# New orders of steps for four of the five blocks of a fused scan, attention and expert kernel

## The reference

```python
x = x + L0_conv(_gn(x))                 # group norm, in_proj, 3x3 depthwise conv, silu, selective scan in 4 directions
t = tokens(x)
t = t + L1_attn(_ln(t))                 # causal attention, 12 heads of 16
t = t + L1_ffn(_ln(t))                  # a second norm, full attention, MLP 192-768-192, then a mixture of 4 experts, top 2
# inside the scan, for each of 4 directions, 96 channels, 16 states, 256 steps:
h = h * exp(d_t * A) + (d_t * u_t) * B_t
y = sum_n(h * C_t)
```

## Time and profile before

| | us |
|---|---|
| median of 3 runs (lowest, highest) | 740.43 (737.93, 743.23) |
| the profiled execution | 742.85 |
| its span in the trace | 741.1 |
| TensorE busy in the span | 608.1 (82%) |
| VectorE busy | 516.4 (70%) |
| ScalarE busy | 321.5 (43%) |
| GpSimd busy | 201.3 (27%) |

### The profile page before, as it was taken

How to read it: one execution, slowest core, us unless ns; L and a number is a source line. 1 busy time by engine, 2 the same in 40 slices (tenths; PEclk the granted TensorE clock), 3 DMA queues, 4 the chain that set the end, 5 groups by cost and what they waited for, 6 DMA issues and landing times. The chain is left out here.

```text
span 741.1 us, 9169 instructions
## 1 busy us (share of the span) xinstructions
PE 608.1 (82%) x3378; PEld 392.0 (53%) x3378; DVE 516.4 (70%) x986; ACT 321.5 (43%) x588; POOL 201.3 (27%) x158
## 2 busy tenths in 40 slices
PE   3899947898737689958898789867996989898897
PEld 2232225455212576645455576645465767676696
DVE  3869746868998578789997478799995465542311
ACT  2334202236353053784572345583761324672241
POOL 4449710005474201053442010153441001000000
PEclk9999968689768799878999789889999999999999
DMA  6375940348772002386750004575620000000000
GB/s 130 40 178 145 278 141 0 44 99 206 185 188 60 11 0 38 80 200 155 178 134 0 22 0 57 144 187 147 181 63 11 0 2 1 0 1 11 1 1 11
DMA packets 26642, 61.70 MB, mean 83 GB/s; under 512 B 4928, under 2 KB 12752, under 8 KB 26608
## 3 DMA queue, kind: packets, MB, share of 16 engines
q1 hardware_dynamic: 26608, 61.26, 34.8%
HBM read 53.52 MB, written 3.54 MB: 77 GB/s over the span
## 5 line engine op out<-in xcount | busy, mean ns | idle before, releaser
L1106 PE MATMUL pd<-w_dn,act 128*128 128x192 f32 x480 | 87.2, 336 | 5.5 <-ACT act L1872 3.7
L1992 POOL TENSOR_TENSOR state<-state,C_rows 128x1024 f32<-128x1024 f32 x24 | 69.8, 2909 | 62.5 <-DVE state L1491 40.6
L1106 PEld LDWEIGHTS pd<-w_dn,act 128*128 128x128 f32 x480 | 80.2, 195 | 11.7 <-issue 6.3
L1090 PE MATMUL pu<-fT,w_up 128*128 128x256 f32 x180 | 61.8, 427 | 7.6 <-ACT act L1872 7.6
L1967 POOL TENSOR_TENSOR norm_rstd<-norm_var,half 128x2 f32<-128x2 f32 x20 | 14.0, 698 | 197.5 <-DVE norm_var L1304 197.5
L1872 ACT ACTIVATE act<-pu,b_up 128x256 f32<-128x256 f32 x90 | 37.7, 470 | 67.4 <-PE pu L1094 67.2
L942 PE MATMUL py<-identb 128*32 128x512 bf16 x224 | 59.1, 412 | 0.0
L1842 ACT ACTIVATE decay<-d_rows,a_neg 128x255 f32<-128x255 f32 x96 | 40.5, 498 | 11.2 <-DVE state L1491 10.3
L1092 PE MATMUL pu<-fT_high,w_up_stack 128*128 128x256 f32 x90 | 45.2, 503 | 0.0
L1032 PE MATMUL py<-state,sel 128*32 128x512 f32 x96 | 43.8, 665 | 1.6 <-POOL state L1992 1.6
L822 PE MATMUL ps<-hT,w_qkv 96*96 96x256 f32 x128 | 35.9, 444 | 9.5 <-ACT hT L1902 8.6
(11 more groups left out here) (310 smaller groups left out, 1384.6 us busy)
## 6 DMA issues: line engine op xcount, KB each, us to landing
dx_rows<-delta_x_dram SPq DMA_DIRECT2D x41, 512.0 KB, 5.2
d_rows<-delta_dram SPq DMA_DIRECT2D x36, 512.0 KB, 6.3
d_rows<-delta_x_dram SPq DMA_DIRECT2D x6, 512.0 KB, 4.8
w_dn<-exp_w_dram SPq DMA_DIRECT2D x1, 2304.0 KB
B_rows<-xdbl SPq DMA_DIRECT2D x4, 512.0 KB, 6.9
C_rows<-xdbl SPq DMA_DIRECT2D x4, 512.0 KB, 10.5
delta_x_dram<-delta_x SPq DMA_DIRECT2D x4, 384.0 KB, 3.4
w_up<-exp_w_dram SPq DMA_DIRECT2D x1, 1536.0 KB
```

Of the source, the lines that this page charges most:

```text
L1090: nc.tensor.matmul(out, w_up[:, e, hidden], fT[:, :], start=True, stop=False)
L1106: mm = nc.tensor.matmul(pd[:, WIDTH * tl:WIDTH * (tl + 1)], act[e % 2][:, m, 128 * tl:128 * (tl + 1)], w_dn[:, e, m, :], start=(m == 0), s ...
L1992: nc.gpsimd.tensor_tensor(now, now, C_rows[:, :], ALU.mult).then_inc(sc_done, 1)
```

## The change

The lists of OPENING, FIRST, STEADY and LAST are written anew; CLOSING stays. No operation is changed. On VectorE, ScalarE and GpSimd the opening keeps its sequence, though the slots are named otherwise, and so does GpSimd in STEADY and LAST. The number of fillers goes from 23 to 28 in the opening, 121 to 76 in FIRST, 29 to 44 in STEADY and 17 to 13 in LAST. The core of the diff:

```diff
@@ -55,90 +55,94 @@
 OPENING = {
     "PE": {
...
-        (0, 1): [("keep_busy", 7)],
-        (0, 3): [("x_dbl", 0), ("x_dbl", 1), ("dt", 0), ("dt", 1), ("keep_beside", 9), ("spread_delta", 0)],
-        (0, 4): [("keep_beside", 1), ("spread_delta_x",), ("spread_delta", 1)],
...
-        (1, 10): [("y_sum", 10), ("keep_beside", 4)],
...
-        (1, "context"): [("keep_beside", 2), ("y_norm",)],
...
+        (0, 1): [("group_sums",), ("in_proj",), ("keep_busy", 7), ("x_dbl", 0), ("x_dbl", 1),
+            ("keep_beside", 1), ("dt", 0)],
+        (0, 2): [("dt", 1), ("keep_beside", 10)],
+        (0, 3): [("spread_delta", 0), ("spread_delta_x",), ("spread_delta", 1)],
...
+        (1, 5): [("spread_delta", 11), ("y_sum", 8), ("y_sum", 9), ("keep_beside", 8)],
...
+        (1, 10): [("keep_beside", 2)],
...
 FIRST = {
     "PE": {
-        (0, "turned"): [("keep_busy", 5), ("x_turn",), ("keep_busy", 6), ("group_sums",)],
-        (0, "projected"): [("in_proj",)],
+        (0, "turned"): [("keep_busy", 6), ("x_turn",), ("keep_busy", 7), ("group_sums",)],
+        (0, 0): [("in_proj",)],
...
-        (0, 9): [("dt", 1)],
-        (0, 11): [("keep_busy", 5)],
-        (0, "spread"): [("keep_busy", 19)],
-        (0, "output"): [("keep_busy", 30)],
-        (1, "projected"): [("keep_busy", 12), ("y_sum", 0), ("keep_busy", 15)],
...
-        (1, 2): [("y_sum", 3), ("y_sum", 4), ("keep_busy", 13)],
-        (1, 3): [("keep_busy", 5)],
...
+        (0, 10): [("dt", 1)],
+        (0, "context"): [("keep_busy", 6)],
+        (0, "output"): [("keep_busy", 27)],
+        (1, 0): [("y_sum", 0)],
+        (1, 1): [("keep_busy", 13), ("y_sum", 1)],
+        (1, 2): [("y_sum", 2), ("keep_busy", 12)],
+        (1, 3): [("y_sum", 3), ("y_sum", 4)],
...
-        (1, 7): [("y_sum", 7), ("y_sum", 8), ("y_sum", 9)],
...
+        (1, 7): [("keep_busy", 5), ("y_sum", 8), ("y_sum", 9)],
...
-        (1, 10): [("keep_busy", 1), ("y_sum", 11), ("keep_busy", 10)],
+        (1, 10): [("y_sum", 11)],
...
     "ACT": {
...
-        (0, 9): [("softplus", 0)],
-        (0, 11): [("softplus", 1)],
-        (0, "context"): [("softplus_log",)],
-        (0, "spread"): [("split_up", 0)],
+        (0, 1): [("in_proj",), ("split_up", 0)],
...
+        (0, 5): [("x_dbl", 1), ("split_up", 1)],
+        (0, 8): [("split_up", 2)],
+        (0, 9): [("softplus", 0), ("softplus", 1)],
+        (0, "output"): [("softplus_log",)],
...
-        (1, "projected"): [("decays", 1), ("split_up", 1), ("decays", 2)],
...
-        (1, 1): [("decays", 5), ("decays", 6), ("split_up", 2), ("decays", 7)],
-        (1, 4): [("split_up", 3), ("decays", 8)],
-        (1, 5): [("split_up", 4)],
-        (1, 6): [("split_up", 5), ("decays", 9), ("decays", 10)],
...
+        (1, 4): [("split_up", 3), ("decays", 7), ("decays", 8), ("decays", 9)],
+        (1, 6): [("split_up", 4), ("split_up", 5), ("decays", 10)],
...
     "POOL": {
...
-        (0, "output"): [("split_up", 0), ("times_C", 0)],
...
-        (1, 2): [("times_C", 3), ("split_up", 1), ("times_C", 4)],
...
+        (1, 2): [("split_up", 0), ("times_C", 2)],
+        (1, 3): [("times_C", 3), ("split_up", 1)],
         (1, 4): [("split_up", 2)],
...
-        (1, 10): [("split_up", 3), ("times_C", 7)],
...
-        (1, "context"): [("y_norm",), ("split_up", 4)],
-        (1, "output"): [("y_out",), ("split_up", 5)],
...
+        (1, 6): [("split_up", 3), ("times_C", 5), ("times_C", 6)],
...
+        (1, 8): [("split_up", 4), ("split_up", 5)],
...
 STEADY = {
     "PE": {
-        (0, "turned"): [("ffn_turn", 0), ("keep_busy", 2), ("x_turn",)],
-        (0, "projected"): [("group_sums",)],
-        (0, 0): [("ffn_up", 0, 0)],
-        (0, 1): [("in_proj",), ("ffn_up", 0, 1)],
-        (0, 2): [("ffn_up", 0, 2), ("ffn_down", 0, 0), ("ffn_down", 0, 1)],
-        (0, 4): [("x_dbl", 0)],
-        (0, 5): [("x_dbl", 1), ("keep_busy", 5), ("ffn_turn", 1), ("dt", 0)],
-        (0, 6): [("ffn_up", 1, 0), ("ffn_logits",)],
-        (0, 7): [("ffn_up", 1, 1)],
-        (0, 8): [("ffn_turn_gates",), ("dt", 1)],
-        (0, "context"): [("ffn_bias",), ("keep_busy", 5)],
-        (0, "spread"): [("ffn_up", 1, 2)],
+        (0, "turned"): [("ffn_turn", 0), ("x_turn",)],
+        (0, "projected"): [("keep_busy", 3)],
+        (0, 0): [("group_sums",)],
+        (0, 1): [("ffn_up", 0, 0), ("in_proj",), ("ffn_up", 0, 1), ("ffn_up", 0, 2)],
+        (0, 2): [("ffn_down", 0, 0)],
+        (0, 3): [("ffn_down", 0, 1)],
+        (0, 4): [("x_dbl", 0), ("keep_busy", 5)],
+        (0, 6): [("x_dbl", 1)],
+        (0, 7): [("dt", 0), ("ffn_turn", 1)],
+        (0, 8): [("ffn_up", 1, 0), ("dt", 1), ("ffn_logits",)],
+        (0, 10): [("ffn_up", 1, 1)],
+        (0, "spread"): [("ffn_turn_gates",), ("keep_busy", 15), ("ffn_bias",), ("ffn_up", 1, 2)],
         (0, "output"): [("ffn_down", 1, 0), ("ffn_up", 2, 0), ("ffn_up", 2, 1)],
         (1, "turned"): [("ffn_up", 2, 2)],
-        (1, "projected"): [("y_sum", 0), ("y_sum", 1), ("ffn_up", 3, 0)],
+        (1, "projected"): [("ffn_up", 3, 0), ("y_sum", 0), ("y_sum", 1)],
         (1, 0): [("ffn_down", 1, 1)],
-        (1, 1): [("y_sum", 2), ("ffn_down", 2, 0)],
-        (1, 3): [("y_sum", 3)],
-        (1, 4): [("ffn_down", 2, 1), ("y_sum", 4), ("ffn_up", 3, 1), ("y_sum", 5)],
-        (1, 6): [("keep_busy", 6), ("ffn_up", 3, 2), ("y_sum", 6), ("y_sum", 7)],
-        (1, 7): [("y_sum", 8), ("ffn_down", 3, 0), ("ffn_down", 3, 1), ("ffn_up", 4, 0)],
-        (1, 8): [("keep_busy", 11), ("ffn_up", 4, 1), ("y_sum", 9), ("ffn_up", 4, 2)],
-        (1, 10): [("y_sum", 10), ("y_sum", 11), ("y_norm",)],
-        (1, 11): [("ffn_down", 4, 0)],
-        (1, "context"): [("y_turn",)],
-        (1, "spread"): [("y_out",), ("ffn_down", 4, 1)],
+        (1, 2): [("y_sum", 2), ("y_sum", 3), ("ffn_down", 2, 0), ("ffn_down", 2, 1)],
+        (1, 3): [("ffn_up", 3, 1), ("keep_busy", 10), ("y_sum", 4), ("y_sum", 5), ("ffn_up", 3, 2)],
+        (1, 4): [("y_sum", 6), ("y_sum", 7)],
+        (1, 5): [("ffn_down", 3, 0), ("keep_busy", 5), ("y_sum", 8), ("keep_busy", 6), ("ffn_down", 3, 1)],
+        (1, 6): [("ffn_up", 4, 0), ("y_sum", 9)],
+        (1, 7): [("ffn_up", 4, 1)],
+        (1, 8): [("ffn_up", 4, 2)],
+        (1, 10): [("y_sum", 10), ("y_sum", 11)],
+        (1, 11): [("y_norm",), ("ffn_down", 4, 0), ("ffn_down", 4, 1), ("y_turn",)],
+        (1, "context"): [("y_out",)],
     },
...
     "DVE": {
...
-        (0, 3): [("silu",), ("ffn_norm", 0)],
-        (0, 4): [("x_dbl", 0), ("ffn_norm", 1)],
...
-        (0, 7): [("ffn_logits",)],
-        (0, 11): [("dt", 1), ("ffn_turn_gates",), ("softplus", 0), ("softplus", 1)],
-        (0, "context"): [("softplus_log",)],
...
+        (0, 4): [("ffn_norm", 0), ("x_dbl", 0)],
+        (0, 6): [("ffn_norm", 1)],
...
+        (0, 9): [("dt", 1), ("softplus", 0)],
+        (0, 10): [("ffn_logits",)],
+        (0, 11): [("softplus", 1)],
+        (0, "context"): [("ffn_turn_gates",), ("softplus_log",)],
...
-        (1, 1): [("ffn_add", 1), ("scan", 5)],
-        (1, 3): [("scan", 6)],
...
-        (1, 5): [("scan", 8), ("ffn_add", 2)],
-        (1, 7): [("scan", 9), ("scan", 10), ("scan", 11)],
-        (1, 9): [("ffn_add", 3), ("y_copy",)],
-        (1, 11): [("y_norm",)],
...
-        (1, "spread"): [("y_out",), ("ffn_add", 4)],
...
+        (1, 2): [("ffn_add", 1)],
+        (1, 3): [("scan", 6), ("scan", 7), ("scan", 8), ("ffn_add", 2)],
+        (1, 4): [("scan", 9)],
+        (1, 5): [("scan", 10)],
+        (1, 7): [("ffn_add", 3), ("scan", 11)],
+        (1, 10): [("y_copy",)],
+        (1, 11): [("y_norm",), ("ffn_add", 4), ("y_turn",)],
...
     "ACT": {
...
-        (0, 8): [("ffn_logits",), ("ffn_up", 1, 1), ("softplus", 0)],
-        (0, "context"): [("softplus", 1), ("softplus_log",), ("ffn_up", 1, 2)],
-        (0, "spread"): [("ffn_up", 2, 0), ("decays", 0)],
-        (0, "output"): [("ffn_up", 2, 1), ("decays", 1), ("ffn_up", 2, 2)],
-        (1, "turned"): [("decays", 2), ("decays", 3)],
...
+        (0, 7): [("softplus", 0)],
...
+        (0, 9): [("softplus", 1), ("ffn_logits",)],
+        (0, 11): [("softplus_log",), ("ffn_up", 1, 1), ("ffn_up", 1, 2), ("ffn_up", 2, 0)],
+        (0, "context"): [("decays", 0), ("ffn_up", 2, 1), ("decays", 1)],
+        (0, "output"): [("decays", 2)],
+        (1, "turned"): [("ffn_up", 2, 2), ("decays", 3)],
         (1, "projected"): [("decays", 4)],
-        (1, 0): [("decays", 5), ("decays", 6)],
-        (1, 4): [("ffn_up", 3, 0), ("decays", 7), ("decays", 8)],
...
-        (1, 6): [("decays", 9), ("ffn_up", 3, 2)],
-        (1, 7): [("decays", 10), ("decays", 11), ("ffn_up", 4, 0)],
+        (1, 1): [("decays", 5), ("ffn_up", 3, 0), ("decays", 6), ("decays", 7)],
+        (1, 3): [("decays", 8), ("ffn_up", 3, 1), ("ffn_up", 3, 2), ("decays", 9)],
+        (1, 5): [("decays", 10), ("ffn_up", 4, 0), ("decays", 11)],
...
 LAST = {
     "PE": {
```

(32 more changed lines are left out.)

233 lines of the change are left out of this document (116 added, 117 removed).

## The result

The changed kernel takes 745.50 us (median of 7 executions, 742.64 to 746.83), the kernel before 741.89 in the same session. The ratio is 1.0051, 95% interval 1.0027 to 1.0074: slower by half a per cent, where 734 us and a gain of 6.8 were predicted. The profiled execution has a span of 743.7 us after 741.1 (745.43 us in all after 742.85).

A forecast was written before the change was run, and what follows sets the result against it. VectorE, taking turns with GpSimd in the scans, was taken as the bound over most of the span. Opening +0.3, first attention block -2.5, middle -3.6, last -1.0 sum to -6.8 us: 734 from 740.43, range 729 to 739.

The forecast's parts named there:

- First attention block, first half: First attention block up to its scan half: in_proj behind row_max 0 gives -1.3 us, moved fillers and earlier softplus 1 -1.0.
- Opening: Opening: fillers moved on TensorE around dt, the spreads and y_sum 10 cost +0.3 us, bounds -0.5 and +2.7.
- First block's scan half: First attention block's scans: more VectorE and GpSimd meetings, and possible waits for row maxima, cost +1.3 us.
- norm_shift: First attention block's end: with split_up moved away, two small operations run freed, norm_shift from 0.93 to 0.16 us; -1.5 us.
- Middle block, first half: Middle block ahead of its scan half: waits for logits and second transpose go, fillers nearly pay for themselves; -1.2 us per pass.
- Scan half 0: Middle block's scans: VectorE keeps its work and its cycle with GpSimd, decays 11 just fit; 0 us per pass.
- Tail: Middle block's end: output leaves before the layer norm, hiding its transfer, and the second ffn_down 4 costs 1.5; -0.6 us per pass.
- Middle block -3.6: Middle block as a whole: -1.8 us per pass, -3.6 for its two passes.
- A: Fifteen fillers ahead of the middle block's output projection run at 1.2 GHz; +3 us per pass, 740 us; chance 0.20.
- B: TensorE bounds the middle block's scan half, at shifted 1, making a late decay delay scan 11; 748 us, mildly 742; chance 0.14.
- C: Fewer meetings of VectorE and GpSimd in the first attention and middle blocks; -8 us, 726 us; chance 0.16.
- D: Whole kernel: a gain in one half is waited away at the next projection; 740 us; chance 0.08.

The follow-up runs named there:

- e4: Changed kernel with TensorE's order of the first attention block's first half as before, other engines' orders staying changed; 742.27 us, 0.9977 of the kernel before.
- e7: Changed kernel with eight more TensorE fillers in the first attention block's first half; 744.18 us, 1.0019 of the kernel before.
- e3: Changed kernel with only in_proj of the first attention block moved back ahead of the scores; 742.44 us, 1.0008 of the kernel before.
- e13: The kernel of e3 again, unedited, for a second profile; 746.13 us.
- e2: Kernel before with only the middle block of the changed kernel; 754.95 us, 1.0147 of the kernel before.
- e12: The kernel of e2 again, unedited, profiled in a later session on another chip; 745.91 us.
- e1: Changed kernel with the whole first attention block of the kernel before; 745.61 us, 1.0042 of the kernel before.
- e5: Changed kernel again, nothing edited, for a second profile; 747.27 us.
- e15: The kernel of e4 with, in the middle block, ffn_up 3,0 behind row_max 0 and in_proj ahead of ffn_up 0,0; 1.0091 of the kernel before.
- e16: The kernel of e7 with ffn_up 3,0 moved behind row_max 0 in the middle block; 739.69 us, 0.9968 of the kernel before.
- e18: The kernel of e16 again, unedited, for a tighter interval; 744.61 us, 1.0026 of the kernel before.
- e17: The kernel of e4 with ffn_up 3,0 behind row_max 0 in the middle block and the eight fillers of e7; 742.57 us, 1.0021 of the kernel before.

## Why the prediction was wrong

*The step that failed* is "First attention block, first half": -1.3 for in_proj, -1.0 for the rest, +5.0 measured. The two edges that it named did what it said. The third stack's copy starts at 120.76 where it was 120.72, although the block had begun 0.76 us and its x_turn another 0.6 later: the 1.3 us of in_proj are there. The wait of 2.35 us went. What failed is the silent assumption behind these sums, that TensorE's clock would be up where it was up before. in_proj, put behind row_max 0, ran at 1.2 GHz (1.91 + 1.86 us), z came 2.0 us later, and from there every step of the half but its end ran at the lower level. e4 and e7, in which the clock came back by 34 us of the block, show the half at 53.4 and 53.5 us. Why the clock misses its rise under the changed order in six of seven profiles stays open: in_proj put back alone (e3, e13) didn't bring it up. The clock appears in that paragraph once, as a bound of 2.1 us on the projection (0.5 measured), not on the 41 us ahead of it. The Trainium skill, page TensorE: Matmul & The Clock Gate, section "What's actually happening", says that the throttled state is the default, and that the monitor runs free of the kernel, so that the ramp varies from run to run. This case's profiles agree that one program varies (e2 against e12: 59.5 and 52.6 us for the half), and the prediction had used only the first of these two statements.

*The other terms.* Opening +0.3: +0.76 measured. First block's scan half +1.3: +1.08 measured, and the multiplies took 0.8 us more than in the earlier trace rows:

```profile
L1499 DVE TENSOR_TENSOR dx_rows<-dx_rows,B_rows 128x1024 f32<-128x1024 f32 x12 | 22.4, 1864 | 1.1 <-DMA dx_rows<-delta_x_dram 1.1
```

norm_shift -1.5: from y_copy to the end of the block 14.5 us for 16.0, so the gain came; but y_copy starts 6.1 us behind the last scan where it started 4.5 behind, with the wait of 1.45 us for row maxima in between that the sum had not counted, and the tail took +0.15. Middle block, first half, -1.2 a pass: +1.71 and -0.90. "0" for in_proj behind ffn_up 0,0 was mis-sized: VectorE waits 2.93 and 2.60 us for z where it waited 1.2 and 1.3. From z to the residual the passes gain 0.5 and 0.7 only: the 0.89 is gone, but 0.25 of the 0.45 stays, and in the first pass 0.62 us stand ahead of the last transpose, which waited for nothing, and 0.55 ahead of the multiply behind it. Scan half 0: -0.42 and -0.46 in this profile, about +2.5 a pass in half of the 26. Tail -0.6: -1.6 in both passes; hiding the transfer was worth 1.9 us of the 2.1 estimated, and of the 1.5 that ffn_down 4 was to give back 0.3 came. Middle block -3.6: the 3.3 of this profile are luck. By the thirteen profiles and the one of the kernel before the gain is near nothing, so this is a second term that the record doesn't bear out. Last block -1.0: -0.67.

*The rivals.* A is out: the fifteen fillers took 3.41 us. B is out at its place: no decay was late by more than 0.5 us. But its mechanism, TensorE as the bound of the scan half once its clock is down, is what gives 73.3 for 70.3 us, ahead of the third stack instead of at shifted 1; its two times, 742 and 748, enclose the 745.50. C: no gain; the multiplies of the first block took longer. D's 740 is 5 us off. None had the clock of the first block. Of the two signs named for "wrong" one came: VectorE idled 7.9 us for row maxima in the first attention block, 3.02 of them at once, while both passes stayed within 1 us of 158. The sum had priced such waits in the scan half; most of them, 5.7 us for 2.2 before, came in the first half, from TensorE's work at the lower clock.

*Why single repairs didn't show.* e1, e4, e7 each took 5.6 to 7.8 us off the first block and the kernel gained 0 to 3.2: the passes' scans went from 70.3 to 73.3 in one or both, as chance or the shifted moment had it; e4 alone is clear of the noise. So that the clock makes the first half long is shown in the profiles (e7), that TensorE's order of that half costs time is shown by e4, and how the 3.6 us of the time share out over the blocks is not. Whether the shift causes the longer scans, or the chance seen in e5 explains all of it, stays open.

## What to carry to other kernels

When an order is changed on an engine whose clock falls and rises on the way, price the whole stretch up to the next rise at both levels, not only the operation that is moved: here 5 us hung on it and the edges moved were worth 1 each. Fillers where short work has gaps early in such a stretch came with the rise in four of four profiles (three of them at the changed order, which had it in one of seven without them), though no kernel with them was shown to be faster than the kernel before. Keep work off the place just ahead of a result that another engine waits for. Profile an unedited kernel several times before a block's time is believed: the middle block's gain of 3.3 us was not there in eleven of twelve more profiles, and the kernel before, with which all are compared, has one.

## What was not expected of the hardware

- The 108 executions of the kernel before that the ratios of the five experiment sessions keep run from 737.5 to 749.4 us; against the granted clock of each, the line of best fit falls by 5.8 us per 0.01 (correlation -0.86). Most of this kernel's spread goes with its clock.
- TensorE stayed at 1.2 GHz while it was busy in 34.0 of 40.9 us (changed kernel) and in 17.3 of 20.6 (e15); in e7 it was busy in 10.9 of the 13.7 us ahead of its rise to 2.4 GHz.
- A program can load its loop anew: 29 loads on the instruction queue instead of 20, the nine more from the end of the first pass on, and TensorE 3.1 and 3.5 us late at its start, in e1 and e2, and not in e12, which is e2's program. The Trainium skill, page Runtime: NRT & Kernel Launch, section "Instruction fetch mechanics", says that a taken branch to code that isn't held forces a fetch; TensorE's idle of 6.85 us in e2, put down to "issue", agrees.
- One kernel measured twice gave 0.9968 and 1.0026 (e16, e18), intervals that overlap only near their ends; the two sessions ran on different chips. One of e17's twelve executions took 1337 us; it is left out, and nothing here explains it.
